# Second attention's follow-up jobs at other steps of its loop, and the mixture layers' normalised rows kept as fp16 halves that DMA transposes for routing and experts

## The chip, the cores and the metric

The kernel runs on one core of one Trainium2 chip. The metric is the device time of one execution in microseconds; lower is better. Three runs of the kernel before gave 951.81, 952.78 and 956.13 us, so its time is 952.78 us.

## The reference

Two layers, each of them a gated cross attention and a gated mixture of experts, on 2048 tokens (8 x 256) of width 256 with a context of 512 rows:

```
x = x + tanh(g_xattn[0]) * attention0(layernorm(x), ctx)     # linear attention with a sigmoid gate
x = x + tanh(g_ffn[0])   * mixture0(layernorm(x))            # 8 experts, best 2, plus a shared expert
x = x + tanh(g_xattn[1]) * attention1(layernorm(x), ctx)     # softmax, 16 heads of 16, q, k, v and weights rounded to 8 bits
x = x + tanh(g_ffn[1])   * mixture1(layernorm(x))            # 16 experts, best 4, plus a shared expert

mixture(x):
    probs = softmax(x @ router.T);  w = top_k(probs), zero elsewhere (layer 0: divided by their sum)
    routed = sum_e w[:, e] * ((silu(x @ gate_e) * (x @ up_e)) @ down_e)            # inner width 176
    shared = sigmoid(x @ s) * ((silu(x @ sgate) * (x @ sup)) @ sdown)              # inner width 704
    return routed + shared
```

## The kernel before, in words

Every engine has its own program, and they meet through semaphores. `at_least(eng, sem, base, n)` (L197) makes an engine wait until a counter has come to base + n; `both` (L284) makes a pair of such counters, one for each mixture layer. Products are exact to nearly fp32: each operand is kept as two fp16 halves, high and low (low = value - high), and `mm3` (L265) adds three fp16 products for each of the two 128-wide parts of the model width.

The stages come one after the other: weights and context, first attention, then for layer 0 routing (L371 to L457), mixture (`ffn_pe`, `ffn_act`, `ffn_dve`, `ffn_pool`, L669 to L1060), then the second attention (`attn1_pe`, `attn1_act`, `attn1_dve`, `attn1_sp`, `attn1_pool`), then routing and mixture of layer 1, then the output.

**Routing.** The 16 tiles of 128 tokens go in 8 pairs. ACT normalises the even tile of a pair (L424), DVE the odd one (L443), into `xnf` as fp32. PE transposes the pair (L380, four fp32 transposes), ACT copies the high half to fp16 (L428), DVE subtracts for the low half (L451), both into `xnT` with the model width on the partitions; PE makes the router's logits from it (L388), DVE scales them (L455). `xnT` is also the shared expert's operand (L778). SP stores the fp32 rows to a table in DRAM (`token_table`, `table_dma`, L632), with the routing weights beside them. From the logits DVE and PE make lists of slots (`route_part_dve`, L603; it begins with MAX8, L465), which run beside the first five steps of the shared expert. `rows_dve` (L564) waits for the stores of rows, since it reuses `xnf`.

**Expert loop.** Slots come in groups of two tiles of 128, each tile of one expert; 20 groups in layer 0, 40 in layer 1 (`NG`). POOL gathers the rows of a group from the table by index (L673), into a ring of `XR` = 4 groups, and a gather waits for the product of the group that held its place (L671). PE transposes the rows (L815, four fp32 transposes), ACT copies the high half (L894), DVE subtracts (L1002); PE does gate and up (L836, twelve products of 352 columns); ACT applies silu (L903); DVE multiplies (L1018); PE transposes the result (L844), ACT and DVE halve it (L907, L1024), PE does down (L852, ten products of 256 columns), DVE copies it out (L1031), SP stores it to the slot table (L658). PE's program handles in step s: the rows' transposes of group s+1, gate and up of s, the result's transposes of s-1, down of s-2. Bank 6 takes the result's transposes, bank 7 the down product. In layer 0 POOL also splits weights of layer 1 into halves between gathers (`split_part`, L1546), and SP loads them (`load_item`, L1539).

**SP's program** is a list in a fixed order (L1594 to L1657): loads, the zeroing of layer 1's slot table in 16 parts (L652), four weight loads (L1644), `table_dma(sp, 0)`, four more loads, `rows_dma(sp, 0)`, loads, the attention's DMA transposes (L1588), `table_dma(sp, 1)`, a wait for the zeroing, `rows_dma(sp, 1)`, the output.

**Second attention.** 128 steps, one for each pair of heads of each tile. In step s PE makes the logits of step s+2 (L1344) into a ring of 5 banks and the weighted sums of step s-4 (L1356); DVE finds the largest logit of each row (L1450); ACT takes exponentials (L1417), and SP transposes them by DMA (L1588). Other work hangs on certain steps, written out by hand as numbers (L1321, `chain_start` L1323, `query_step`, `output_step`): for every two tiles the queries of a later pair (POOL's rows, PE's transposes, ACT's high and DVE's low half, PE's product, DVE's largest value, scale and fractions, POOL's rounding and cutting, PE's transposes back, ACT's copies) and the output of an earlier one (PE's transposes L1365, ACT's high half L1423, DVE's low half L1465, PE's projection, DVE's update of x L1471, and statistics). An engine that comes to such a job before its operand is there waits, with all that is behind it.

## Time and profile before

| what | value |
|---|---|
| median of 3 runs | 952.78 us |
| the profiled execution: its time | 959.28 us |
| its span, first to last instruction | 957.5 us |
| granted TensorE clock, mean | 0.843 of full |
| instructions | 18420 |

Instants in the rows below count from the start of the span. The profiled execution took somewhat longer than the median; sums are made against it and then moved to the median. PE is TensorE's matmul side, PEld its weight loads, DVE VectorE, ACT ScalarE, POOL GpSimd, SP SyncE; SPq and POOLq are their DMA-issuing instructions. A granted clock of 1.00 is 2.4 GHz, 0.50 is 1.2 GHz.

### The profile page before, as it was taken

What the parts mean: (1) busy time and instruction counts of PE and PEld (TensorE: products, weight loads), DVE (VectorE), ACT (ScalarE), POOL (GpSimd) and SP (SyncE); (2) the same over time, 40 slices, a digit from 0 to 9 for tenths busy, and PEclk for the clock granted to TensorE, in tenths of its full rate; (3) what the DMA queues carried; (4) which work ended last, traced back from release to release, by engine and by line L of the source; (5) the groups of instructions that cost most, each with busy time, mean ns of one, the idle gap of its engine ahead of it and who ended that gap; (6) DMA issues with size and microseconds to landing.
All of it is one profiled execution on the core that took longest, in us unless ns stands there. A gap on an engine that the chain in (4) does not pass through costs nothing.

```text
span 957.5 us, 18420 instructions
## 1 busy us (share of the span) xinstructions
PE 746.1 (78%) x5700; PEld 496.1 (52%) x5701; DVE 686.8 (72%) x1825; ACT 443.4 (46%) x1037; POOL 505.3 (53%) x607
## 2 busy tenths in 40 slices
PE   3469749678988797677777777659879999977994
PEld 1258635456664454344444444335657777754563
DVE  4868947756775777988887888738857777734467
ACT  3355335123332233888887878725123444422331
POOL 6284974566636557553554347010054545478883
PEclk9679876789999899697767676657979999978998
DMA  8034444624542213898889988821034444446444
GB/s 287 1 92 157 157 157 147 187 80 142 164 127 89 66 34 81 146 191 160 151 163 168 182 159 162 148 75 40 0 93 137 136 136 140 142 123 143 79 79 141
DMA packets 205754, 121.17 MB, mean 127 GB/s; under 512 B 146476, under 2 KB 197808, under 8 KB 205680
## 3 DMA queue, kind: packets, MB, share of 16 engines
q1 hardware_dynamic: 192816, 91.10, 39.2%
q0 software_dynamic: 12864, 29.14, 12.5%
q8 instruction: 38, 0.62, 0.3%
q14 instruction: 36, 0.29, 0.1%
HBM read 64.16 MB, written 32.98 MB: 101 GB/s over the span
## 4 chain that ended last, share of the span: by engine, by line
PE 35%; DVE 11%; ACT 7%; issue 6%; DVEq 4%; DMA 3%; another core or an unknown queue 2%; POOL 1%; POOLq 0%; ACTq 0%
PE PS L269 18%; PE PS L852 4%; DVE sb_wk L1450 4%; PE PS L791 3%; ACT sb_xnf L1417 3%; DMA sb_xnf<-sb_xnf 3%; PE PS L1344 2%; ACT sb_wkh L1417 2%; PE PS L815 2%; PE PS L844 2%; PE PS L407 1%; DVEq L250 1%; DVE sb_x_sb L942 1%; DVE sb_x_sb L948 1%
## 5 line engine op out<-in xcount | busy, mean ns | idle before, releaser
L673 POOL DMA_INDIRECT sb_xnf<-token_table,sb_ids x120 | 115.8, 965 | 148.7 <-DVE sb_wk L1018 62.8
L1450 DVE TENSOR_SCALAR_CACHE_REDUCE sb_wk<-PS 128x512 f16<-128x512 f32 x256 | 161.9, 684 | 3.8 <-PE PS L1344 3.8
L269 PE MATMUL PS<-sb_xnT,sb_sgu 128*128 128x512 f16 x528 | 129.5, 398 | 1.1 <-DVE sb_lg L455 0.6
L269 PE MATMUL PS<-sb_region,sb_wkh 128*128 x720 | 122.6, 321 | 4.8 <-issue 3.1
L1417 ACT ACTIVATE sb_xnf<-PS,sb_slotv 128x512 int16<-128x512 f32 x128 | 86.8, 689 | 25.5 <-DVE sb_wk L1450 21.4
L875 ACT ACTIVATE sb_wk<-PS 128x512 f32<-128x512 f32 (+1 forms) x48 | 28.6, 596 | 144.6 <-PE PS L269 123.7
L269 PEld LDWEIGHTS PS<-sb_region,sb_wkh 128*128 128x128 f16 x720 | 69.7, 100 | 47.0 <-issue 13.9
L1417 ACT ACTIVATE sb_wkh<-PS,sb_slotv 128x512 int16<-128x512 f32 x128 | 86.6, 690 | 12.4 <-DVE sb_wk L1450 9.6
L852 PE MATMUL PS<-sb_region,sb_wkh 128*128 x600 | 78.3, 277 | 8.9 <-DVE sb_wa L1031 7.3
L269 PEld LDWEIGHTS PS<-sb_xnT,sb_sgu 128*128 128x128 f16 x528 | 53.0, 102 | 60.7 <-issue 10.9
L791 PE MATMUL PS<-sb_sdn,sb_wkh 128*128 128x256 f16 x544 | 70.8, 282 | 17.4 <-DVE sb_wkh L989 15.2
L1018 DVE SCALAR_TENSOR_TENSOR sb_wk<-PS,sb_sm,sb_wk 128x176 f32<-128x176 f32 x120 | 42.6, 396 | 54.2 <-ACT sb_wk L903 41.2
L1344 PE MATMUL PS<-sb_wa,sb_xnf 128*128 128x512 f16 x88 | 43.0, 489 | 44.6 <-ACT sb_wkh L1417 22.2
L894 ACT ACTIVATE sb_wkh<-PS 128x512 f16<-128x512 f32 x60 | 35.8, 596 | 85.4 <-PE PS L815 48.3
L791 PEld LDWEIGHTS PS<-sb_sdn,sb_wkh 128*128 128x128 f16 x544 | 54.2, 101 | 37.5 <-DVE sb_wkh L989 20.1
L903 ACT ACTIVATE sb_wk<-PS 128x352 f32<-128x352 f32 x60 | 27.8, 463 | 95.8 <-PE PS L269 74.1
L981 DVE SCALAR_TENSOR_TENSOR sb_wk<-PS,sb_wk 128x512 f32<-128x512 f32 (+1 forms) x48 | 33.2, 691 | 53.9 <-ACT sb_wk L875 44.0
L852 PEld LDWEIGHTS PS<-sb_region,sb_wkh 128*128 128x128 f16 x600 | 56.7, 99 | 21.9 <-issue 12.6
L1561 POOL TENSOR_TENSOR sb_region<-sb_stg,sb_region 128x704 f16<-128x704 f32 (+1 forms) x32 | 42.9, 1340 | 19.9 <-issue 17.1
L1002 DVE TENSOR_TENSOR sb_wkh<-PS,sb_wkh 128x512 f16<-128x512 f32 x60 | 41.1, 685 | 17.1 <-ACT sb_wkh L894 13.6
L1739 POOL TENSOR_SCALAR sb_xnT<-sb_xnT 128x256 f32<-128x256 f32 x16 | 7.3, 456 | 85.0 <-DVE sb_xnT L1288 85.0
L815 PE MATMUL PS<-sb_idf,sb_xnf 128*128 128x128 f32 x240 | 38.9, 287 | 16.7 <-DMA sb_xnf<-token_table,sb_ids 16.7
(296 smaller groups left out, 1717.3 us busy)
## 6 DMA issues: line engine op xcount, KB each, us to landing
slot_table<-sb_wa SPq DMA_DIRECT2D x60, 256.0 KB
slot_table<-token_table SPq DMA_DIRECT2D x16, 640.0 KB
sb_stg<-gu SPq DMA_DIRECT2D x24, 352.0 KB
sb_stg<-dn SPq DMA_DIRECT2D x24, 256.0 KB
token_table<-sb_xnf SPq DMA_DIRECT2D x16, 256.0 KB, 4.7
sb_stg<-sgu SPq DMA_DIRECT2D x8, 352.0 KB
sb_x_sb<-x SPq DMA_DIRECT2D x1, 2048.0 KB, 12.3
out<-sb_x_sb SPq DMA_DIRECT2D x16, 128.0 KB
```

What stands on the lines that cost most here:

```text
L269: last = nc.tensor.matmul(out_, lhs(i, c), rhs(j, c), start=(c == 0 and n == 0 and not begun), stop=(c == C - 1 and n == 2 and not more))
L673: nc.gpsimd.indirect_dma_start(xg[l][:, 2 * (g % XR) + n, :], None, xw[l][:, :], bass.IndirectOffsetOnAxis(ap=ids[:, 2 * g + n:2 * g + n + ...
L791: last = nc.tensor.matmul(PS[:, first + i // 2, i % 2 * D:(i % 2 + 1) * D], wkh[:, HR * h + v, i * P:(i + 1) * P], sdn[:, j, k, :], start= ...
L815: last = nc.tensor.transpose(PS[:, 4 + s % 2, (2 * n + c) * P:(2 * n + c + 1) * P], xg[l][:, 2 * (s % XR) + n, c * P:(c + 1) * P], idf[:, :])
L852: last = nc.tensor.matmul(PS[:, 7, n * D:(n + 1) * D], wkh[0:r, 4 + 2 * u + i, (2 * c + n) * P:(2 * c + n + 1) * P], DN[l][0:r, bass.ds(e[ ...
L894: nc.scalar.activation(wkh[:, 2 * (s % 2), :], PS[:, 4 + s % 2, :], ACT.Copy).then_inc(e_xh[l].sem, 1)
L1002: nc.vector.tensor_tensor(wkh[:, 2 * (s % 2) + 1, :], PS[:, 4 + s % 2, :], wkh[:, 2 * (s % 2), :], ALU.subtract).then_inc(e_xl[l].sem, 1)
L1018: last = nc.vector.scalar_tensor_tensor(wk1[:, 2 + u, n * EI:(n + 1) * EI], PS[:, 2 * u + n, EI:EG], wv[u][:, n:n + 1], wk1[:, u, n * EI:( ...
L1344: nc.tensor.matmul(PS[:, (2 * s + h) % LB, :], q_iT[t % 3][:, pair, :], keys, start=True, stop=True).then_inc(h_qk, 1)
L1417: nc.scalar.activation(h_count[s % 4][:, h * CTX:(h + 1) * CTX], PS[:, (2 * s + h) % LB, :], ACT.Exp, scale=-1.0, bias=h_nb[u][:, h:h + 1] ...
L1450: nc.vector.tensor_scalar(h_any[(2 * s + h) % 6], PS[:, (2 * s + h) % LB, :], LEVELS, None, ALU.add, ALU.min, accum_out=h_nb[s % 3][:, h:h ...
L1561: nc.gpsimd.tensor_tensor(lo, w, hi, ALU.subtract).then_inc(stg_split[n % 4], 1)
```

## The change

**Rows as halves.** In routing, both engines normalise into `wk1` (ring of four pairs); ACT copies the high half and DVE subtracts the low half as rows, side by side in `xnf` as fp16 (`x_rows`, the same bytes as one fp32 row). SP transposes each pair by one DMA transpose, 128 x 1024 fp16, into `xnT` (seen as `x_cols`), and only after all eight come the stores of rows. PE's logits wait for the transposes; four banks take them, and DVE scales them four pairs later. PE's transposes go.

```diff
+            for j in range(NT // 2):
+                at_least(pe, x_turned[j % 4][l], 0, 16 * (j // 4 + 1))
+                at_least(pe, r_lgc[l], 0, j - 3)
+                for i in range(2):
+                    t = 2 * j + i
+                    last = mm3(PS[:, j % 4, i * n:(i + 1) * n], lambda h, c: x_cols[:, t, h, c, :],
+                               lambda h, c: rw[l][:, h, c, :])
+                last.then_inc(r_lg[l].sem, 1)
...
         def table_dma(sp, l):
             for j in range(NT // 2):
-                at_least(sp, r_xn[l], 0, j + 1)
-                at_least(sp, r_xd[l], 0, j + 1)
+                at_least(sp, r_xh[l], 0, j + 1)
+                at_least(sp, r_xl[l], 0, j + 1)
+                at_least(sp, x_turned[j % 4][l], 0, 16 * (j // 4))
+                sp.dma_start_transpose(x_turns[:, 2 * j:2 * j + 2].rearrange("p t g n -> p (t g) n"),
+                                       x_rows[:, 2 * j:2 * j + 2].rearrange("p t h n -> p (t h n)")).then_inc(x_turned[j % 4][l].sem, 16)
+            for j in range(NT // 2):
                 sp.dma_start(token_rows(xw[l], 2 * j, 2, slice(0, D)), xnf[:, 2 * j:2 * j + 2, :]).then_inc(stored[l].sem, 16)
```

**Expert loop.** The gathered rows are halves already. SP transposes them by DMA, two of 128 x 512 fp16 for each group, into a ring of four (`xT`), four groups ahead of the store of the group's result. PE's four transposes of the rows, ACT's copy and DVE's subtraction go. The result's transposes take two banks in turn (5 and 4), the down product two (6 and 7), and PE's waits on them are one group later. The wait for the zeroing moves behind the first four of layer 1's transposes.

```diff
         def rows_dma(sp, l):
+            def turn(g):
+                at_least(sp, e_ld[l][g % XR], 0, 32 * (g // XR + 1))
+                at_least(sp, e_gu[l], 0, g + 1 - XR)
+                if g == 0:
+                    at_least(sp, s_d[l], 0, HALF)
+                for n in range(2):
+                    sp.dma_start_transpose(xT[g % XR][:, 2 * C * n:2 * C * (n + 1), :],
+                                           xg[l][:, 2 * (g % XR) + n, 0:D].bitcast(F16)).then_inc(e_xT[l][g % XR].sem, 16)
+            for g in range(XR):
+                turn(g)
+            if l == 1:
+                sp.wait_ge(table_zeroed, 16 * ZERO_PARTS)
             for g in range(NG[l]):
+                if g + XR < NG[l]:
+                    turn(g + XR)
                 at_least(sp, e_y[l], 0, g + 1)
                 sp.dma_start(ys[l][2 * g * P:(2 * g + 2) * P, :].rearrange("(n p) d -> p n d", p=P),
                              yb[g % 2].rearrange("p (n d) -> p n d", n=2)).then_inc(e_st[l][g % 2].sem, 16)
...
             def group(base, s):
                 u = s % 2
-                if inside(base, s, 0, NG[l] - 1):
-                    transposes(base, s + 1)
                 if inside(base, s, 0, NG[l]):
                     e = experts(base, s)
-                    at_least(pe, e_xl[l], base, s + 1)
+                    at_least(pe, e_xT[l][s % XR], base * 8, 32 * (s // XR + 1))
...
-                at_least(pe, e_hl[l], base, s - 1)
+                at_least(pe, e_hl[l], base, s - 2)
...
                 if inside(base, s, 2, NG[l] + 2):
                     e = experts(base, s - 2)
-                    at_least(pe, e_y[l], base, s - 2)
+                    at_least(pe, e_hl[l], base, s - 1)
+                    at_least(pe, e_y[l], base, s - 3)
```

**Second attention.** Only the steps at which jobs are issued, and places in `xnT` so that jobs that now overlap have their own.

```diff
-        ROWS, TO_PE, HIGH_Q, LOW_Q, PRODUCTS, LARGEST, SCALES, FRACTIONS, PARTS, BACK, COPIES = 0, 1, 2, 3, 4, 7, 8, 10, 10, 12, 13
+        ROWS, TO_PE, HIGH_Q, LOW_Q, PRODUCTS, LARGEST, SCALES, FRACTIONS, PARTS, BACK, COPIES = 0, 1, 1, 4, 3, 7, 8, 10, 10, 10, 11
...
-            return max((GSTEPS - 1) * (G - 1), GSTEPS * (G - 1) - 4)
+            return max((GSTEPS - 2) * (G - 1), GSTEPS * (G - 1) - 4)
```

Of the output's jobs PE's transposes and ACT's high half go from step 6 to 5, DVE's low half from 7 to 8, PE's projection from 8 and 9 to 7 and 8, DVE's update from 10 to 11, its statistics from 11 and 12 to 12 and 15.

## Rows read from the trace of the kernel before

**Rows 1.** The page: busy time, share of the span and instructions of each engine.

```profile
PE 746.1 (78%) x5700; PEld 496.1 (52%) x5701; DVE 686.8 (72%) x1825; ACT 443.4 (46%) x1037; POOL 505.3 (53%) x607
```

**Rows 2.** Stages: start:end, us, busy of PE, PEld, DVE, ACT, POOL, PEclk, DMA share, GB/s.

```profile
195.00:292.00 97.00, 85.66 (x614) 61.61 (x615) 62.16 (x161) 33.04 (x81) 55.17 (x56) 0.96 0.44 131
373.00:634.00 261.00, 186.14 (x1675) 105.29 (x1673) 213.08 (x648) 201.38 (x543) 116.39 (x178) 0.73 0.85 155
637.00:653.00 16.00, 12.03 (x130) 9.44 (x131) 9.88 (x35) 9.96 (x17) 0.79 (x1) 0.50 0.38 133
...
695.00:845.00 150.00, 142.34 (x1078) 109.45 (x1079) 110.67 (x291) 59.99 (x144) 74.89 (x81) 0.97 0.44 131
845.00:882.00 37.00, 24.41 (x135) 14.84 (x133) 13.32 (x31) 6.26 (x16) 29.68 (x29) 0.77 0.56 130
```

**Rows 3.** Line 1031, DVE's copy of a group's result: layer 0, then layer 1 to 845.

```profile
L1031 DVE COPY sb_wa<-PS x20: 690/692/693, 211.0 to 288.9; 128x512 f32<-128x512 f32 x20
...
L1031 DVE COPY sb_wa<-PS x33: 690/692/692, 717.4 to 843.5; 128x512 f32<-128x512 f32 x33
```

**Rows 4.** The chain of waits in layer 1's expert loop: start, us, what.

```profile
839.90 1.34 PE PS L269 x9
...
841.68 1.10 PE PS L852 x10
842.77 0.44 PE PS L815 x4
```

**Rows 5.** Waits: us in all, times, longest; 205 to 285 (two rows), 705 to 845.

```profile
POOL sb_region L1561 <- issue: 15.1, 6, 3.5
...
POOL sb_xnf L673 <- DVE sb_wk L1018: 1.1, 2, 0.9
...
POOL sb_xnf L673 <- DVE sb_wk L1018: 61.7, 35, 2.8
```

**Rows 6.** Timeline around layer 0's routing: start, us, engine, line.

```profile
154.56 0.17 DVE L455 TENSOR_SCALAR sb_lg<-PS 128x18 f32<-128x18 f32 x1 [0.49 <-PE PS L269]
...
158.37 5.31 SPq L1541 DMA_DIRECT2D sb_stg<-gu  x1
...
165.82 2.26 SPq L637 DMA_DIRECT2D token_table<-sb_xnf  x3
...
169.98 0.78 POOL L1556 TENSOR_SCALAR sb_region<-sb_stg 128x704 f16<-128x704 f32 x1 [13.20 <-DMA sb_stg<-gu]
...
179.51 1.15 DVE L572 TENSOR_TENSOR sb_wa<-sb_region,sb_slotc 128x640 f16<-128x640 f16 x1 [2.34 <-DMA token_table<-sb_xnf]
```

**Rows 7.** DMA, 600 to 622: queue, packets, MB, share; issues to landing; one issue.

```profile
q1 hardware_dynamic: 12764, 3.17, 83.7%
...
sb_xnf<-sb_xnf SPq DMA_TRANSPOSE x7, 3.3
...
606.88 1.23 SPq L1588 DMA_TRANSPOSE sb_xnf<-sb_xnf  x1
```

**Rows 8.** Timeline of layer 1's routing: the first pair, the last logits.

```profile
640.00 0.60 ACT L428 ACTIVATE sb_xnT<-PS 128x512 f16<-128x512 f32 x1 [0.73 <-PE PS L380]
...
640.63 0.69 DVE L451 TENSOR_TENSOR sb_xnT<-PS,sb_xnT 128x512 f16<-128x512 f32 x1 [1.92 <-ACT sb_xnT L428]
...
651.96 0.19 DVE L455 TENSOR_SCALAR sb_lg<-PS 128x34 f32<-128x34 f32 x1 [0.49 <-PE PS L269]
```

**Rows 9.** DMA queues in layer 1's expert loop, 700 to 840: packets, MB, share.

```profile
q0 software_dynamic: 3489, 10.11, 26.9%
q1 hardware_dynamic: 8704, 8.39, 17.4%
```

**Rows 10.** Second attention: DVE's waits, 400 to 620; line 1450, all of it.

```profile
DVE sb_x_sb L1471 <- PE PS L275: 15.4, 7, 3.0
...
DVE sb_xnT L1465 <- ACT sb_xnT L1423: 6.1, 6, 2.5
...
L1450 DVE TENSOR_SCALAR_CACHE_REDUCE sb_wk<-PS x256: 627/685/693, 375.2 to 620.4; 128x512 f16<-128x512 f32 x128
```

More of the change, by code:

```diff
@@ L289, in gated_flamingo @@
         r_xn = both("r_xn", NT // 2)
-        r_xT = both("r_xT", NT // 2)
+        x_turned = [both(f"x_turned{u}", 32) for u in range(4)]
         r_xh = both("r_xh", NT // 2)
@@ L333, in gated_flamingo @@
         e_ld = list(zip(*(both(f"e_ld{u}", 32 * len(range(u, NG[0], XR))) for u in range(XR))))
+        e_xT = list(zip(*(both(f"e_xT{u}", 32 * len(range(u, NG[0], XR))) for u in range(XR))))
         e_st = list(zip(*(both(f"e_st{u}", 16 * len(range(u, NG[0], 2))) for u in range(2))))
@@ L351, in gated_flamingo @@
         yr = [xnf_flat[:, r * 2 * D:(r + 1) * 2 * D].rearrange("p (k d) -> p k d", d=D) for r in range(CR)]
-        y_sum = [w[:, n * D:(n + 1) * D] for w, tiles in ((stg_flat, 8), (wqp32, 4), (xnf_flat[:, 12 * D:16 * D], 4))
+        y_sum = [w[:, n * D:(n + 1) * D] for w, tiles in ((stg_flat, 8), (wqp32, 4), (wkv32, 4))
                  for n in range(tiles)]
@@ L364, in token_rows @@
             return ap[r:r + n * P, cols].rearrange("(n p) d -> p n d", p=P)
+        LOGITS_LATE = 4
         CHOICES = 1
@@ L809, in ffn_pe @@
             at_least(pe, r_ids[l], 0, 1)
-            def transposes(base, s):
-                at_least(pe, e_ld[l][s % XR], base * 8, 32 * (s // XR + 1))
-                for n in range(2):
-                    for c in range(C):
-                        last = nc.tensor.transpose(PS[:, 4 + s % 2, (2 * n + c) * P:(2 * n + c + 1) * P],
-                                                   xg[l][:, 2 * (s % XR) + n, c * P:(c + 1) * P], idf[:, :])
-                last.then_inc(e_xT[l].sem, 1)
             def experts(base, s):
@@ L843, in group @@
                         for c in range(C):
-                            last = nc.tensor.transpose(PS[:, 6, (2 * c + n) * P:(2 * c + n + 1) * P],
+                            last = nc.tensor.transpose(PS[:, 5 - u, (2 * c + n) * P:(2 * c + n + 1) * P],
                                                        wk1[:, 3 - u, n * EI + c * P:n * EI + (c + 1) * P], idf[:, :])
@@ L856, in group @@
                     last.then_inc(e_d[l].sem, 1)
-            transposes(0, 0)
             steps(pe, NG[l] + 2, XR, XR, 3, group)
@@ L890, in ffn_act @@
                     nc.scalar.activation(numbers[l], bc(io[:, 0:P], NT), ACT.Copy).then_inc(r_numbers[l].sem, 1)
-            def high_x(base, s):
-                at_least(act, e_xT[l], base, s + 1)
-                nc.scalar.activation(wkh[:, 2 * (s % 2), :], PS[:, 4 + s % 2, :], ACT.Copy).then_inc(e_xh[l].sem, 1)
             def group(base, s):
                 u = s % 2
-                if inside(base, s, 0, NG[l] - 1):
-                    high_x(base, s + 1)
                 if inside(base, s, 0, NG[l]):
@@ L1013, in group @@
                 if inside(base, s, 0, NG[l] - 1):
-                    low_x(base, s + 1)
+                    weights(base, s + 1)
                 if inside(base, s, 0, NG[l]):
@@ L1093, in gated_flamingo @@
         q_iT = [w.bitcast(F16).rearrange("p (g n) -> p g n", n=P) for w in
-                (*(xnf[:, 12 + 2 * u:14 + 2 * u, :].rearrange("p t d -> p (t d)") for u in range(2)), xn32[:, 10 * D:12 * D])]
+                (*(xnf[:, 12 + 2 * u:14 + 2 * u, :].rearrange("p t d -> p (t d)") for u in range(2)), xn32[:, 14 * D:16 * D])]
         h_h = [wkh[:, 2 * u:2 * u + 2].rearrange("p a b -> p (a b)") for u in range(4)] + \
```

109 lines of the change are left out of this document (47 added, 62 removed).

## The prediction

> **What bounds the kernel now.** I read the busy totals first: no engine is busy all the time, PE the longest [rows 1]. The table of stages then shows why: in the first mixture layer's expert loop (195 to 292 us) and the second's (695 to 845) PE is nearly always busy, at a granted clock of 0.96 and 0.97 of full speed; in the second attention (373 to 634) DVE, ACT and the DMA engines are each between 0.77 and 0.85 busy, and none is full; and where layer 1's tokens are normalised (637 to 653; layer 0's stage is alike) PE runs at clock 0.50, and only 16 us are at stake [rows 2]. The stages follow each other, so what one loses moves the end by as much.
>
> Third, for each loop, who waits. In layer 1 a group takes (843.5 - 717.4)/32 = 3.94 us [rows 3], and PE's links in the chain follow each other without a gap, 0.149 us for a gate/up product, 0.110 for one of the down projection, 0.44 for four fp32 transposes [rows 4]. Twelve, ten and twice four of them are 3.77 us of 3.94: PE is the bound. POOL has slack there: it waits 61.7 us for DVE. In layer 0 a group takes 77.9/19 = 4.10 us by the same rows of the copy, and POOL waits for DVE for 1.1 us only, but 15.1 us ahead of its own third part of a weight split [rows 5]: there POOL, which gathers rows and splits weights in turn, sets the pace, and PE waits for gathers.
>
> **Part 1, routing in layer 0: slower.** This is the largest term. Today the logits need PE transposes, ACT and DVE, and the last is scaled at 154.56 us. The row stores of SP are behind in time: SP is held by the zeroing of the slot table and then by four weight loads until 165.82, when the first store of rows goes out; that it went out so late cost nothing until 179.51, where DVE waited 2.34 us for the stores [rows 6]. The change puts eight DMA transposes in the place of these stores, at the same point of SP's program, and now the logits need them. They can't be issued before 165.82. The queue is backed up too: the load issued at 158.37 landed at 169.98 [rows 6], and three more loads stand behind it, so I let the first transpose run at about 170. One of 128 x 1024 fp16 took 0.837 x 22 us / (3.17 MB / 0.25 MB) = 1.45 us of all 16 DMA engines in the attention, 3.3 us from issue to landing, with 1.23 us on SP's queue [rows 7]. Eight are 11.6 us, so the last is done at about 182, lands by 183, and with PE's last logits and DVE's scale the routing ends near 184: 29.4 us later than 154.56. The 2.34 us wait for the stores goes, since they have some 20 us of route to land in. Net **+26.5**. Bounds: without backlog 1.5 us of SP per transpose gives 165.8 + 8 x 1.23 + 3.3 = 179 (+22); if the loads ahead hold the queue until 173, +31.
>
> **Part 2, routing in layer 1: a little slower.** Here SP is free. ACT and DVE keep their work per pair of tiles (a copy of 0.60 us, a subtraction of 0.69 and a normalising each [rows 8], with SBUF for PSUM as the source); PE loses four transposes, the queue gains 1.45 us per pair. Without PE's step the first low half is ready somewhat ahead of today's 640.63 + 0.69 [rows 8], and its transpose runs from about 640.8; 8 x 1.45 = 11.6 gives 652.4, some 2 us to land and 0.7 for logits and scale: 655 against 651.96 today [rows 8]: **+3**. Bounds 0 (ACT and DVE pace it and the tail is short) and +6. The later row stores are hidden: 30 us of routing follow.
>
> **Part 3, fill of the two expert loops: +2.** A gather lands, then two transposes of half size take 1.45 us of DMA and about 3.3 to land [rows 7], in place of PE's 0.44, ACT's 0.60 and DVE's 0.69 us and the hand-overs between them [rows 4, 8]. One microsecond each; bounds 0 and +4 together.
>
> **Part 4, expert loop of layer 1: faster.** PE loses the four transposes of the rows, 0.44 us per group: 3.94 to 3.50 us. ACT loses a copy of 0.60, DVE a subtraction of 0.69: neither was the bound. The doubled banks for the second transposes and the down product take away waits that hardly show. What takes PE's place is DMA: the queues carried (0.269 + 0.174) x 140 us over 35.5 groups = 1.75 us per group [rows 9]; with 1.45 of transposes it is 3.20 us, 91% of 3.50. The attention held 0.85 over 261 us [rows 2] and never had to be full. The ring of four stands it: from DVE's product of a group to the products four groups on there are two gathers (about 4.5 us), two transposes (3.3 to 4.7), then 1.8, 0.6 and 0.8 for PE, ACT and DVE, 11 to 13 us, or 2.8 to 3.2 per group. On SP's queue a group's two transposes (about 0.65 us each) stand ahead of the store of four groups before, whose data is later than the gather; that costs nothing. I take 3.58 us: 0.36 x 33 groups = **-12**. Bounds -15 (PE alone) and +3 (DMA at 0.85 share sustained: 3.20/0.85 = 3.76, and the end of the loop worse). The 37 us after 845, where DVE, ACT and PE stand still at clock 0.77 [rows 2], I leave alone: no wait there is for what changes.
>
> **Part 5, expert loop of layer 0: +2.** POOL paces it, and POOL's work is the same; PE's 0.44 us there only ends a wait sooner. DMA goes from 0.44 [rows 2] to about 0.44 + 1.45/4.1 = 0.8, and POOL's drains, which stood 15.1 us in six splits, get longer if gathers land later. Bounds -4 (the last groups at PE's pace) and +8.
>
> **Part 6, the attention: faster.** Queue order only. DVE waited for PE at the update 15.4 us in 7 turns, for ACT at the low half 6.1 us in 6 [rows 10]; the change lets PE project a step earlier and DVE take the low half one and the update one step later (and the query chain's low half too). Both waits should go: for 8 turns some 24 us of DVE time. What is late next: DVE's own work. From 375.2 to 620.4 us are 128 steps of 1.92 [rows 10]; DVE is busy 0.82 of the stage and ACT 0.77, DMA 0.85 [rows 2]. Should DMA go no higher than 0.92, then 8% of 245 us, 19 us, is all there is. The new order has PE take the query transposes two steps sooner after POOL has cut them, and PE wait for DVE's low half at a step that DVE reaches later than before; some of the gain goes there. I take **-10**, with bounds -19 and 0.
>
> **The sum.** 26.5 + 3 + 2 - 12 + 2 - 10 = +11.5 us. The profiled execution took 959.28 us around its span of 957.5, so it would be 971 in it; the median of the runs is 952.78, so I predict **964 us**. About 0.5% (4.8 us) is what a measurement of this kernel can tell from no change.
>
> **A rule against a row.** A transpose of 256 KB took 1.45 us of the DMA engines, a store of the same bytes 0.174 x 140 / (8.39 / 0.25) = 0.73 [rows 7, 9]. The Trainium skill (Advanced Engine Details and Errata, X-Bar Transpose) says that transpose DMAs are as fast as regular ones. The row speaks against it.
>
> **Rivals.**
> *The order on SP does not bind layer 0* (the other side). If transposes reached the queue as the halves come, at 141 us and on, routing would cost +3 as in layer 1: 11.5 - 23.5 = -12, 941 us. It decides from a first issue before about 154, where part 1 falls to +15. Against it: SP is busy with zeroing and loads that nothing in the change moves [rows 6]. Chance 0.07.
> *All gains arrive.* PE-bound layer 1 (-15), attention to the DMA's limit (-19), layer 0's end -2: 26.5 + 3 + 2 - 15 - 2 - 19 = -4.5, 948 us (just inside no change). For it: PE's links without gaps [rows 4] and waits that all sit at the moved steps [rows 10]. Chance 0.15.
> *DMA saturates.* Gathers, stores and transposes share 16 engines: layer 1's loop +3, layer 0's +8, attention -5: 26.5 + 3 + 4 + 3 + 8 - 5 = +39.5, 992 us; halfway 978. For it: 91% wanted. Chance 0.14.
> *Transposes at the rate of a store*, 0.73 us: part 1 less 8 x 0.72 = 5.8, part 2 at 0, layer 1 at -15, layer 0 at 0: 20.7 + 0 + 2 - 15 + 0 - 10 = -2.3, 950 us. Against it stands the 1.45 [rows 7]. Chance 0.03. It is what the rule above would give.
> My forecast has 0.61, and its own range is 953 to 974.
>
> **How the numbers follow.** Range 945 to 980: it takes in the forecast, the second and fourth rivals nearly whole and half of the third. Slower by over 0.5% (above 957.5): 0.57 of the forecast and the third rival, 0.71. Within 0.5%: most of the second rival, the fourth, 0.04 of the forecast, 0.18. Faster: the first and a part of the second, 0.11.
>
> **What would show it.** Layer 0: SP issues the first transpose near 166 us, and the first MAX8 of routing comes near 184, not 154.8; if it comes before 160, part 1 is wrong and with it the sign. Layer 1: the normalising and the logits take some 3 us longer than today. Layer 1's groups at 3.5 to 3.65 us, DMA share near 0.9, clock still near 1; if PE waits for DMA there and groups take 3.9 or more, DMA has saturated. Layer 0's groups at 4.1 or more. Attention: no wait at DVE's update, 1.80 to 1.87 us per step; if PE waits for POOL's or DVE's query steps instead, the stall has moved.

## The result and the profile after

The changed kernel takes 1009.92 us (median of four runs, 1004.68 to 1010.55) against 952.29 us for the kernel before (951.72 to 956.13). By the means of the runs it takes 1.058 times as long, interval 1.054 to 1.063; all ratios below are of means too, each against runs of the kernel before on the same chip. The direction was as predicted. The size was not: +57.6 us for a forecast of +11.5, beyond the range's upper end of 980. Two profiles below, g2's and f1's, are of slow executions (1018.94 and 1020.70 us, where the fastest of each took 1003.56 and 1003.02); behind the last gather of rows, outside the stages that are compared, they take 14 and 12 us more than the changed kernel's.

First the page's busy totals and then the table of stages of the changed kernel, in the columns of [rows 2]: both expert loops, the attention, layer 1's normalising, and layer 1's expert loop where it is steady.

```profile
PE 703.5 (70%) x5396; PEld 456.3 (45%) x5397; DVE 647.8 (64%) x1765; ACT 408.1 (40%) x977; POOL 505.0 (50%) x607
...
213.00:322.00 109.00, 79.09 (x546) 54.02 (x545) 54.30 (x147) 21.69 (x61) 57.64 (x59) 0.94 0.69 166
402.00:683.00 281.00, 189.86 (x1666) 109.37 (x1666) 213.93 (x650) 202.83 (x544) 117.44 (x177) 0.71 0.78 144
683.00:700.00 17.00, 3.90 (x96) 3.19 (x96) 8.85 (x24) 9.39 (x17) 0.00 (x0) 0.50 0.82 151
770.00:895.00 125.00, 104.33 (x759) 72.34 (x760) 70.96 (x205) 30.22 (x87) 54.90 (x59) 1.00 0.77 189
```

The change took off what it meant to: 43 us of PE, 39 of DVE, 35 of ACT [rows 1]. But PE, which was busy for 95% of layer 1's loop [rows 2], is now busy for 104.33 of 125 us, 83%. The work left, and holes came. The attention, 261 us before, is 281 us with the same work on DVE and ACT and a DMA share that fell from 0.85 to 0.78.

The copies of the expert groups' results (line 1031 before, 1029 now) and the attention's maxima (line 1450 before, 1448 now) give the time of each stage, as [rows 3] and [rows 10] did:

```profile
L1029 DVE COPY sb_wa<-PS x20: 691/692/693, 232.1 to 317.3; 128x512 f32<-128x512 f32 x20
...
L1029 DVE COPY sb_wa<-PS x30: 691/692/693, 769.7 to 894.3; 128x512 f32<-128x512 f32 x30
...
L1448 DVE TENSOR_SCALAR_CACHE_REDUCE sb_wk<-PS x256: 627/686/693, 402.1 to 665.0; 128x512 f16<-128x512 f32 x128
```

A group of layer 0 takes 85.2/19 = 4.48 us (4.10 before), one of layer 1 124.6/29 = 4.30 (3.94), an attention step 262.9/128 = 2.05 (1.92). The ledger, in us, each stage by its first or last instruction in the two traces:

| stage | before | after | difference | predicted |
|---|---|---|---|---|
| layer 0: first MAX8 of the routing | 154.8 | 184.3 | +29.5 | +29.4 |
| its routing, MAX8 to first gather | 37.2 | 28.7 | -8.5 | -2.3 |
| layer 0's experts and the rest to the attention | 183.2 | 189.1 | +5.9 | +2, +1 of the fills |
| attention, first to last maxima | 245.2 | 262.9 | +17.7 | -10 |
| its end and layer 1's routing to its last MAX8 | 33.0 | 36.4 | +3.4 | +3 |
| last MAX8 to layer 1's last gather of rows | 190.6 | 201.5 | +10.9 | -12, +1 |
| last gather to the end of the span | 113.5 | 105.9 | -7.6 | 0 |

The sum is 51.3 us of span. The last line is put down to the one execution of the kernel before that was profiled: 959.28 us against a median of 952.78, with a stall in its tail (last section). Without it the ledger gives 58.9, near the 57.6 of the medians. The line before it is touched by the same: the profiles with that stall also have the shorter groups in layer 1, so that like with like, as shown below, the loop lost some 5 to 7 us and not all of 10.9.

### The profile page after: what moved, and what is told of

It is laid out like the page before. It is cut to its first block, busy times and chain, and to the rows that moved or that the text cites. A ratio compares the mean times of both kernels' runs of the same rounds, so it can differ in the third digit from the quotient of the medians.

```text
span 1008.8 us, 17861 instructions
## 1 busy us (share of the span) xinstructions
PE 703.5 (70%) x5396; PEld 456.3 (45%) x5397; DVE 647.8 (64%) x1765; ACT 408.1 (40%) x977; POOL 505.0 (50%) x607
## 4 chain that ended last, share of the span: by engine, by line
issue 25%; POOL 22%; PE 19%; POOLq 8%; DMA 7%; SPq 7%; DVE 6%; ACT 2%; DVEq 2%; ACTq 0%
PE PS L269 11%; PE PS L861 4%; POOL sb_region L731 3%; SPq L656 3%; POOL sb_region L1559 2%; POOL sb_xnf L691 2%; DMA sb_xnf<-token_table,sb_ids 2%; POOLq L1558 2%; DMA sb_xnT<-sb_xnf 2%; POOL sb_stg L731 2%; POOLq L1662 2%; DMA sb_wkh<-sb_xnf 2%; SPq L666 2%; PE PS L852 1%; POOL sb_stg L1556 1%
## 5 line engine op out<-in xcount | busy, mean ns | idle before, releaser
L1448 DVE TENSOR_SCALAR_CACHE_REDUCE sb_wk<-PS 128x512 f16<-128x512 f32 x256 | 164.5, 685 | 48.0 <-PE PS L1342 41.1
L269 PE MATMUL PS<-sb_xnT,sb_sgu 128*128 128x512 f16 x528 | 126.1, 391 | 1.1 <-DVE sb_lg L455 0.6
L1016 DVE SCALAR_TENSOR_TENSOR sb_wk<-PS,sb_sm,sb_wk 128x176 f32<-128x176 f32 x120 | 42.6, 396 | 109.5 <-ACT sb_wk L905 109.5
L269 PE MATMUL PS<-sb_region,sb_wkh 128*128 x360 | 62.7, 328 | 43.7 <-DMA sb_wkh<-sb_xnf 32.0
L809 PE MATMUL PS<-sb_sdn,sb_wkh 128*128 128x256 f16 x544 | 68.3, 276 | 14.7 <-DVE sb_wkh L989 12.8
L861 PE MATMUL PS<-sb_region,sb_wkh 128*128 x600 | 76.5, 273 | 2.8 <-DVE sb_wkh L1024 1.7
L269 PE MATMUL PS<-sb_region,sb_xnf 128*128 x360 | 60.4, 319 | 21.4 <-issue 10.8
L269 PEld LDWEIGHTS PS<-sb_region,sb_wkh 128*128 128x128 f16 x360 | 35.0, 101 | 69.0 <-issue 51.1
L861 PEld LDWEIGHTS PS<-sb_region,sb_wkh 128*128 128x128 f16 x600 | 53.9, 97 | 17.2 <-issue 7.2
L269 PEld LDWEIGHTS PS<-sb_region,sb_xnf 128*128 128x128 f16 x360 | 34.0, 99 | 44.8 <-issue 29.1
L269 PE MATMUL PS<-sb_rw,sb_xnT 128*128 128x9 f16 (+1 forms) x192 | 7.7, 173 | 65.1 <-DMA sb_xnT<-sb_xnf 65.1
```

The lines of the kernel that those rows point to most:

```text
L269: last = nc.tensor.matmul(out_, lhs(i, c), rhs(j, c), start=(c == 0 and n == 0 and not begun), stop=(c == C - 1 and n == 2 and not more))
L809: last = nc.tensor.matmul(PS[:, first + i // 2, i % 2 * D:(i % 2 + 1) * D], wkh[:, HR * h + v, i * P:(i + 1) * P], sdn[:, j, k, :], start= ...
L861: last = nc.tensor.matmul(PS[:, 6 + u, n * D:(n + 1) * D], wkh[0:r, 4 + 2 * u + i, (2 * c + n) * P:(2 * c + n + 1) * P], DN[l][0:r, bass.d ...
L1016: last = nc.vector.scalar_tensor_tensor(wk1[:, 2 + u, n * EI:(n + 1) * EI], PS[:, 2 * u + n, EI:EG], wv[u][:, n:n + 1], wk1[:, u, n * EI:( ...
L1448: nc.vector.tensor_scalar(h_any[(2 * s + h) % 6], PS[:, (2 * s + h) % LB, :], LEVELS, None, ALU.add, ALU.min, accum_out=h_nb[s % 3][:, h:h ...
```

## Layer 0's routing, and the experiment on SP's order

SP's own timeline of the changed kernel (start, us, engine queue, line, destination<-source): zeroing of the slot table, four weight loads, the eight transposes, then the row stores.

```profile
140.91 18.14 SPq L656 DMA_DIRECT2D slot_table<-token_table  x4
159.09 7.35 SPq L1539 DMA_DIRECT2D sb_stg<-gu  x4
166.54 15.06 SPq L638 DMA_TRANSPOSE sb_xnT<-sb_xnf  x8
181.65 6.08 SPq L641 DMA_DIRECT2D token_table<-sb_xnf  x8
```

The first transpose goes out at 166.54 (166 predicted, [rows 6] had 165.82), the eight take 15.06 us of the queue, and the first MAX8 comes at 184.3. The backlog that was forecast is there: the first two transposes hold the queue for 3.3 us each, the other six for 1.27. The first lands at 174.4 and the last at 183.5 (183 predicted). The instant was right to 0.1 us, with a little luck: the transposes started later than at 170 and went faster than one in 1.45 us.

**c1_order** calls the transposes right behind the loads of layer 0's experts, and the zeroing behind the whole loop of layer 0:

```
             two_experts(0, s)
-            for n in range(4):
-                zero_slots(sp, 4 * s + n)
+        turn_rows(sp, 0)
         ...
         rows_dma(sp, 0)
+        for n in range(ZERO_PARTS):
+            zero_slots(sp, n)
```

> The changed kernel with layer 0's eight DMA transposes of rows on SP's queue straight after the loads of layer 0's experts, ahead of the four weight loads, and with all sixteen parts of the zeroing after layer 0's expert loop. Theory, SP's order holds the routing: the first transpose is issued near 142 us, the logits end near 158 in place of 184, and the whole is 22 to 29 us shorter than 1009.9, about 984. Rival, the transposes themselves are slow there (DMA busy with loads): the logits end after 170 and less than 15 us come back. If the zeroing costs as much in the stage after the expert loop as it did before, the routing ends near 158 and the whole still gains less than 15.

992.72 us, ratio 1.043 (1.033 to 1.052). The first MAX8 comes at 154.9 (154.8 before), the first gather at 187.4 instead of 213.0: SP's order was the whole of this term. Some of it was lost again: with the zeroing's traffic ahead of the attention's loads, DVE waited once for 10.5 us at the attention's start, and the stage took 270.6 us.

## The attention: five experiments

The part's two gains were to come from waits of DVE at the update and the low half [rows 10]. Both are gone from the table of waits. These are the waits of the changed kernel from 425 to 660 us (who waits, for what; us in all, times, longest):

```profile
DVE sb_wk L1448 <- PE PS L1342: 39.0, 31, 2.8
...
PE PS L1251 <- POOL sb_xnT L1751: 17.4, 7, 3.2
```

Line 1251 is PE's transposes of the query parts back (step BACK), line 1751 is POOL's cut of the query into integers. PE reaches the transposes at step 10 before POOL has cut, stands there for 2.5 us on the mean, seven times, and behind it in PE's order stand the products that DVE's maxima need. DVE's wait moved from the update to the maxima and grew.

**a1_all_steps_old** puts back all steps of queries and outputs and the chain's start; **a2_query_old** only those of the queries and the chain's start; **a3_back_late** only BACK, COPIES and the start; **g2_chain_old** only the start:

```
-ROWS, TO_PE, HIGH_Q, LOW_Q, PRODUCTS, ..., BACK, COPIES = 0, 1, 1, 4, 3, ..., 10, 11
+a1, a2: 0, 1, 2, 3, 4, ..., 12, 13    a3: 0, 1, 1, 4, 3, ..., 12, 13
-            return max((GSTEPS - 2) * (G - 1), GSTEPS * (G - 1) - 4)
+            return max((GSTEPS - 1) * (G - 1), GSTEPS * (G - 1) - 4)     (all four)
-output_step(s, 5), 7 + j, 5, 8, 11, 12 + 3 * j
+output_step(s, 6), 8 + j, 6, 7, 10, 11 + j     (a1 only)
```

> The changed kernel with every job of the second attention back at its step of before (only the places in memory stay new). Theory, the steps are to blame: the attention, from DVE's first to last search for the largest logit, took 245.2 us before and 262.9 after; here it is 244 to 248 again and the whole about 18 us shorter than the changed kernel's 1009.9, some 992. Rival, the rest of the change (places, DMA, clock) slowed it: it stays at 258 or more and the whole near 1010.

> Only the query chain's steps (from ROWS to COPIES, and the start of the chain) back; the output's jobs stay at their new steps. Theory, PE now comes to the query transposes before POOL has cut the queries, and that is the whole loss, while the output's new steps do what was forecast: the attention takes 228 to 238 us, less than the 245.2 of before, and the whole is 980 to 986. Rival, the projection two steps after the transposes makes PE wait for DVE's low half: the attention stays above 250.

> Query transposes and copies back at steps 12 and 13 and the chain's start at 15 per group as before; the query's high half (1), low half (4) and product (3) and all output jobs stay new. If the early transposes back are the loss: the attention is as in the run with the whole query chain old, within 3 us. If PE's wait for the query's low half at step 3 costs too: it is slower than that run by the difference, 5 us or more.

> The changed kernel with the chain's start of before ((GSTEPS - 1) * (G - 1)) and all else as changed, BACK and COPIES at 10 and 11. If the early transposes back, which come before POOL has cut the query, are the loss: attention 262 as after, ratio 1.055 to 1.06. If it is the denser chain: attention 245 as with both taken back, ratio 1.04. (The other half, the new start with BACK at 12, can't be had: groups then overtake one another's buffers.)

| kernel | attention, us | ratio to before |
|---|---|---|
| the changed kernel | 262.9 | 1.058 (1.054 to 1.063) |
| g2: chain's start old | 259.8 | 1.051 (1.042 to 1.059) |
| a3: and BACK, COPIES at 12, 13 | 245.1 | 1.039 (1.033 to 1.045) |
| a2: and high half, low half and product old | 237.5 | 1.029 (1.024 to 1.035) |
| a1: and outputs old | 242.5 | 1.038 (1.028 to 1.049) |

Read as differences of the stage: the earlier BACK and COPIES cost 14.7 us, the denser chain 3.1, the low half behind the product (with the earlier high half, which a2 moves too) 7.6, and the output steps gain 5.0. Each stage is of one profile, a1 to a3 on one chip and g2 on another, so the 3.1 and the split that g2 makes are the least sure. The row of g2 that decides is the same wait, still there with the old start of the chain:

```profile
PE PS L1251 <- POOL sb_xnT L1751: 15.6, 9, 3.2
```

In a3 it is gone. The other half alone, the new start with BACK at 12, has no run: the query groups would then need one another's buffers in a circle.

**a4_before_outputs_2** is the kernel before with the six output steps of the change and nothing else.

> The kernel before with the new steps of the output's jobs in the second attention and nothing else of the change. The run with all steps old took 242.5 us for the attention, the one with these steps 237.5: so 5 us less than before, ratio 0.995 (0.990 to 0.999). If the gain belongs to the new places in memory or to the change in the mixture, the ratio is 1.00.

943.77 us against 951.95, ratio 0.990 (0.986 to 0.994): it beats both kernels, the kernel before by 1%. Its maxima run from 375.0 to 613.4, 238.4 us instead of 245.2, and the two waits of [rows 10] fell from 15.4 us in 7 turns and 6.1 in 6 to one each from 400 to 640 us:

```profile
DVE sb_x_sb L1471 <- PE PS L275: 3.3, 1, 3.3
...
DVE sb_xnT L1465 <- ACT sb_xnT L1423: 1.8, 1, 1.8
```

## The expert loops: ten experiments

The chain in layer 1's loop of the changed kernel (start, us, what). Line 269 is gate and up, 852 the hidden transposes, 861 down:

```profile
823.50 0.44 PE PS L852 x4
823.94 1.18 PE PS L861 x10
825.12 0.66 issue
825.77 1.96 PE PS L269 x12
```

PE's blocks are 1.96, 0.44 and 1.10 to 1.18 us, and a hole of about 0.6 us stands ahead of gate and up, where before the four transposes stood and the chain had no gap. Two theories. A: the operand is late (gather, SP's queue, landing). B: the hole is TensorE's reading of the two expert numbers into registers (line 832 now, 822 before), which stands right ahead of gate and up and was covered by the transposes.

The read of this group is in the trace, on the side of the weight loads (min, median, max ns, first and last start):

```profile
L832 PEldq TENSOR_LOAD <-sb_texp x1: 761/761/761, 824.9 to 824.9; - x1
```

It runs from 824.9 to 825.6, and gate and up start at 825.77. That is B. There are two such reads a group; over 28 groups in the steady part they took, in the kernel before, in the changed kernel, and in two of the kernels below, b1 and b2:

```profile
L822 PEldq TENSOR_LOAD <-sb_texp x56: 535/547/840, 726.7 to 834.7; - x56
...
L832 PEldq TENSOR_LOAD <-sb_texp x56: 538/782/1032, 775.7 to 893.6; - x56
...
L830 PEldq TENSOR_LOAD <-sb_texp x56: 535/546/906, 765.6 to 874.7; - x56
...
L839 PEldq TENSOR_LOAD <-sb_texp x56: 536/667/994, 774.7 to 888.2; - x56
```

Times per group below are 28 intervals of the copies in the steady part (4.27 us for the changed kernel). One code's loop is not always as long: that of the kernel before took 3.94 us in its profile and 4.10 in a4's, that of the changed kernel 4.27, 4.21 to 4.24 in a1 to a3, and 4.13 in g2. The short ones, 3.94 and 4.13, are from profiles with the stall of the last section. So like with like the loop lost 0.11 to 0.19 us a group (4.21 to 4.27 against 4.10, 4.13 against 3.94), and not the 0.36 between the two profiles above. Where possible, kernels are compared within one chip.

**b1_no_turns_2** leaves out the transposing DMAs after the first four groups (all later groups take the rows of the first four again), **b5_one_turn_2** one of each group's two, **b2_aside_2** sends layer 1's to a place that nobody reads, from a source that is long ready:

```
             for g in range(NG[l]):
-                if g + XR < NG[l]:
-                    turn(g + XR)
```

> The changed kernel with DMA transposes of rows for the first four groups of each mixture layer only; the products of all later groups read these four again, so the routed part of the output is made from the wrong rows. Everything else, the gathers too, stays. Theory A, the operand comes late (SP issues two transposes of 1.26 us and a store per group in a fixed order, and DMA has to land them): without them PE never waits at gate and up, and layer 1's groups fall from 4.15 us (steady part) to 3.5 to 3.6. Theory B, PE's own program is the limit: it loads the experts' numbers into registers ahead of gate and up, which the four transposes of before covered, and the 0.6 us hole ahead of gate and up stays: 4.0 us or more. In layer 0 by theory A 4.48 falls to the 4.1 of before or below.

> As the changed kernel, but in layer 1 the DMA transposes of groups 4 to 39 read constant weights and write to unused memory, at the same instants and of the same size, and PE reads the first four groups' operands again (so layer 1's routed part is made from wrong rows). Same DMA and SP work as the changed kernel, no dependence of PE on it. If it is PE's dependence on late transposes: 3.5 to 3.7 us per group. If it is the DMA load (gathers and stores slowed by the transposes): 4.1 us as in the changed kernel.

> The changed kernel with one DMA transpose per group in place of two: the second tile's product reads the first tile's rows, so the routed part is made from wrong rows for every second tile. SP is busy 1.26 + 0.36 us per group instead of 2.9, DMA 0.73 us less. If the time from a store to the landing of the transposes behind it sets the pace: each group loses a third of 1.26 us or more, 3.7 us or less per group in layer 1. If PE's register loads do it: 4.0 or more.

On one chip: 3.95 us without transposes (ratio 1.040, 1.036 to 1.044), 4.09 with one (1.049, 1.046 to 1.053), 4.11 with both aside (one run, 1006.2 us), and 4.10 for a4, whose loop is that of before. Neither theory stands alone. Most of the hole is there with no transposing DMA at all (B): against a4, b1 is rid of PE's transposes, 0.44 us a group, and gains 0.14. The hole grows with the transposes' traffic though nothing waits for it: 0.16 us. The rows of the reads show how: their mean is 0.61 us in b1 and 0.70 in b2, two a group, which is the 0.16. In layer 0, b1 took 3.92 us a group for 4.48.

**e1_loads_before_turns** reads both pairs of numbers between gate/up and the hidden transposes, **e2_loads_after_turns** between these and down, **e3_loads_no_turns** is e1 without transposing DMAs:

```
         def group(base, s):
+            e = experts(base, s - 2) ...
+            e_next = experts(base, s + 1) ...
             (hidden transposes of s - 1; e2: the two reads stand here)
             (down of s - 2, with e)
+            gate_up(base, s + 1, e_next)
```

> The changed kernel with TensorE's two loads of expert numbers moved: both pairs (down's of the group two back, gate and up's of the next group) are read between a group's gate and up products and its hidden transposes, so that neither stands between down's ten products and the next gate and up. State of the theories: layer 1's groups took 3.945 us before (717.4 to 839.7, 31 intervals), 4.297 after (769.7 to 894.3, 29), 3.943 without the operand transposes (764.7 to 883.0, 30), 4.107 with one a group or with both aside; PE's work is 1.96 + 0.44 + 1.10 = 3.50, and without any transposing DMA a hole of 0.45 still stands ahead of gate and up. Theory B (the hole is the loads' register time, covered before by four transposes, and longer the busier the DMA is): the hole goes, groups 3.55 to 3.7, span shorter by 40 x 0.5 + 20 x 0.4 = 28 us, ratio 0.972 of after, near 1.029 of before. Theory A (the hole is the operand that comes late through gather, SP's turn and landing): groups stay at 4.2 to 4.3, ratio 1.058 of before.

> As the run before, but both pairs of numbers are read after the hidden transposes, right ahead of down. If a load needs only cover by whatever TensorE has queued, this place is as good: 3.55 to 3.7 a group. If what covers it must be long (two microseconds of gate and up rather than 0.44 of transposes), a hole of 0.2 to 0.5 opens ahead of down and groups take 3.8 to 4.1. Theory A: 4.2 to 4.3.

> The first of these two with the transposing DMAs after the first four groups left out, so that the routed part is worked out from wrong rows. It bounds what the loop can reach with the loads covered: theory B 3.50 to 3.6 a group in layer 1 and the same in layer 0 where TensorE's clock is full; the difference to the run with the transposing DMAs is what their queue, landing and traffic cost then. If groups stay at 3.94, the hole is neither the operand nor the place of the loads, and both theories fall.

The hole follows the reads. PE's waits from 773 to 887 us, of e1 (line 854 is the hidden transposes) and then of e2 (862 is down); nothing is left at gate and up:

```profile
PE PS L854 <- issue: 13.1, 26, 1.3
...
PE PS L854 <- DVE sb_wk L1020: 1.4, 1, 1.4
```

```profile
PE PS L862 <- issue: 16.5, 22, 1.6
...
PE PS L862 <- DVE sb_wkh L1028: 7.1, 4, 1.9
```

4.07 us a group in e1, 4.46 in e2, 3.91 in e3; ratios 1.054 (1.050 to 1.059), 1.064 (1.059 to 1.068) and 1.032 (1.027 to 1.036). So it is the reads, but neither place hid them: my 3.55 to 3.7 was wrong. Twelve products of 0.15 us ahead of them did not cover them.

**f1_no_loads** has constant expert numbers (every group uses the last two experts) and no reads; **f2_before_no_loads** is that on the kernel before; **f3_loads_by_four** reads the twelve numbers of a turn of the loop at once; **f4_neither** is f1 without transposing DMAs after the first four groups:

```
-            return nc.values_load_multi_w_load_instructions(texp[0:1, j], ...)[1]
+            return E[l] - 2, E[l] - 1          (f1, f2, f4)
+            if s % XR == 0:                    (f3)
+                v = read(bass.ds(base * 2 + 2 * (s - 2), 2 * (XR + 2)))
```

> The changed kernel with constant expert numbers in both expert loops (the last two experts for every group, so that the routed part is worked out with wrong experts), hence no loads of numbers into TensorE's registers. If the loads are the hole (0.7 us a group in layer 1): groups of 3.50 to 3.65 there and 3.5 to 3.7 in layer 0 where the clock is full, 25 to 40 us off the span, ratio 1.02 to 1.03 of before. If the hole is the operand's way (gather, SP's turn, landing) after all, groups stay above 4.0.

> The kernel before with the same constant numbers. If its four operand transposes covered the loads, little is won: groups of 3.945 become 3.88 to 3.94 (its work is 1.96 + 0.44 + 1.10 + 0.44 = 3.94 with ends that overlap), ratio 0.99 to 1.0. If the loads cost TensorE their time wherever they stand, groups fall by 0.4 or more and the ratio is below 0.98.

> The changed kernel with the numbers of one turn of the loop (four steps, and the two ahead of them for down) read in one load of 12 registers at the turn's first gate and up; three steps in four have no load. If a load's cost is a latency each time: a hole of 1 to 1.5 us in every fourth step, groups of 3.75 to 3.95 on the mean, some 15 to 20 us off the span. If it goes by the number of registers, 12 against 16 a turn: 4.1 to 4.2.

> The changed kernel with constant expert numbers and without the transposing DMAs after the first four groups (routed part worked out from wrong experts and wrong rows). With the loads and the transposes a group of layer 1 took 4.28, without the transposes 3.94, without the loads 4.23. If these two are all that held the loop above TensorE's own 3.50, groups take 3.50 to 3.55, the ratio is 1.00 to 1.02 of before, and TensorE is busy for over 98% of the loop. If a third thing holds it (the chain through ACT and DVE back to TensorE), groups stay above 3.7.

The copies of g2 (the change's own expert loop, same chip), f1, f3 and, on another chip, f4:

```profile
L1029 DVE COPY sb_wa<-PS x29: 691/692/694, 772.6 to 888.2; 128x512 f32<-128x512 f32 x29
```

```profile
L1027 DVE COPY sb_wa<-PS x29: 691/692/694, 786.2 to 892.9; 128x512 f32<-128x512 f32 x29
```

```profile
L1039 DVE COPY sb_wa<-PS x29: 691/692/695, 775.1 to 884.1; 128x512 f32<-128x512 f32 x29
```

```profile
L1025 DVE COPY sb_wa<-PS x29: 691/692/694, 760.1 to 860.0; 128x512 f32<-128x512 f32 x29
```

Over 28 intervals: 4.13 us with reads and transposes, 3.81 without reads, 3.89 with reads by four, 3.57 with neither. The reads are worth about 0.3 us a group and the transposing DMAs another 0.24. f1's figure is the least steady: by which 28 intervals are taken it is 3.78 to 4.01, f3's is 3.80 to 3.91, the other two move by 0.04 at most. So f1 and f3 can't be told apart. f1 also spares TensorE the addresses worked out from the numbers, which f3 keeps, so that f3's 0.24 is the reads alone.

A third limit is left. The chain of f2, the kernel before without reads, is PE's own work and nothing else (line 842 is the hidden transposes there, 850 down, 815 the rows' transposes):

```profile
807.01 1.79 PE PS L269 x12
808.80 0.44 PE PS L842 x4
809.24 1.10 PE PS L850 x10
810.34 0.44 PE PS L815 x4
```

Without the last line it is 3.33 us, and f4 is 0.24 above that. Between the first of its hidden transposes and of its down products PE takes 0.60 us in f4 and 0.44 in f2: there it waits for ACT and DVE, which halve the result. That f4 comes to the 3.58 that I had forecast for the whole change is chance. In f1 the limit that stood behind the reads comes forward. Its waits at gate and up name the DMA, and its chain runs through SP's queue (lines 666: a half-size transpose, 676: the store of a group):

```profile
829.49 0.36 SPq L676
...
829.95 1.22 SPq L666
831.17 0.04 issue
831.21 1.27 SPq L666
832.48 0.04 issue
832.52 0.58 SPq L676
```

```profile
PE PS L269 <- DMA sb_wkh<-sb_xnf: 8.2, 6, 3.3
...
PE PS L269 <- DMA sb_xnf<-sb_xnf: 3.8, 4, 1.2
```

So theory A is true as well, one step behind B. A group wants 0.4 to 0.6 + 1.22 + 1.27 us of SP's queue, about 3 us.

The control on the kernel before: f2 took 3.76 us a group where [rows 3] had 3.94, ratio 0.990 (0.985 to 0.995), so even there the reads cost, 0.17 us. Against a4's 4.10 it would be 0.33; f2's profile has the stall, as the one of before, so I take the 0.17. The ratios of f1, 1.047 (1.042 to 1.051), f3, 1.052 (1.047 to 1.058), and f4, 1.022 (1.018 to 1.026), fell short of what was expected of them: the last six groups took 33 to 40 us in these profiles for 20 in the changed kernel's (last section), and the attention's and layer 0's losses are all still in. f1's layer 0 even took 4.75 us a group for 4.48.

**Two sums of parts.** **c3_query_old_loads** joins a2, e1 and c1 with the zeroing put right behind layer 0's transposes; **h1_outputs_loads** is a4 with f3's reads by four.

> The change's parts that earn, put together: the output steps new, the query steps and the chain's start as before, layer 0's eight row transposes issued right after the loads of layer 0's experts, the zeroing of the slots behind them and ahead of the weights' items (not in the attention as in the run that moved it there, whose first stretch had a stall of 10.5 us), and the loads of expert numbers early. From after's 1009.9: query steps -29.6 as measured, routing -25.6 at the first gather of layer 0 as measured, and by theory B -28: 927 us, ratio 0.973 (0.96 to 0.99). By theory A: 955, ratio 1.003.

> The kernel before with the output jobs' new steps (alone 0.9898 of before) and with the expert numbers of four steps read in one load. Taking the loads away on the kernel before gave 0.9895 (3.855 a group in layer 1 against 3.945). If the reads by four win half of that and it adds up: ratio 0.985 (0.980 to 0.990). If one load of twelve registers opens a hole as long as those it replaces: 0.990 to 0.993.

c3 took 1035.3 us, ratio 1.087 (1.083 to 1.092), the slowest of all. Its timeline of SP says why:

```profile
156.39 80.07 SPq L658 DMA_DIRECT2D slot_table<-token_table  x16
236.52 7.33 SPq L1545 DMA_DIRECT2D sb_stg<-gu  x4
243.90 6.46 SPq L643 DMA_DIRECT2D token_table<-sb_xnf  x8
```

The sixteen pieces of zeroing, 5 us of queue each, spread between weight loads in the kernel before, now stand together ahead of the row stores that the routing waits for, and TensorE, DVE, ACT and POOL all stand still from 180 to 240 us. The rest went as its parts: attention 234.4 us, 4.07 a group. h1 took 951.21 against 959.82, ratio 0.990 (0.986 to 0.994), no more than a4 alone. Its groups took 3.80 us and its last gather of rows came at 835.4, 6.4 us before a4's, but its tail took 114.0 us for a4's 106.8, with the stall of the last section in it.

## Why the prediction was wrong

**Part 1** (layer 0's routing, +26.5): the mechanism and its instant were right (184, measured 184.3; c1 undoes it). The term was too large by 5.5, since I let only the 2.34 us of one wait go. The route itself became 8.5 us shorter. The wait is gone, and DVE's same 117 instructions take 23.67 us of it for 29.98, where POOL, which splits weights, is busy for 1.09 us instead of 15.26. Of line 572's two, one took 1147 ns before and 479 the other, and 484 and 492 after. That POOL is the cause was not tested.

**Part 2** (+3) and **part 3** (+2): right, +3.4 and within what can't be told from the loops.

**Part 4** (layer 1's experts, -12) failed, and with a wrong sign: +10.9 in the ledger, some 5 to 7 like with like. The step was "twelve, ten and twice four of them are 3.77 us of 3.94: PE is the bound", from which I took the 0.44 of the transposes off. By that sum PE's work without them is 3.33 us. The other 0.17 us was there to be read, was left unexplained, and stayed in the 3.50. It was the part of the register reads that stuck out from under the transposes (f2: 3.76 without reads). With the transposes gone about 0.3 us of them stuck out, and behind them the operand came late: 4.27 us a group where I forecast 3.58. A second step was "about 0.65 us each" on SP's queue for a half-size transpose: it took 1.26, as much as the full size in [rows 7]. A third was to let DMA cost nothing below a share of 0.85 to 0.92: its share was 0.77 in the changed kernel's loop, yet the transposes' traffic cost 0.16 us a group where nobody waited for them (b2), by longer reads.

**Part 5** (+2): 4.10 to 4.48 us a group, +7.3 over 19 groups, by the same things: 3.92 without the transposes. My upper bound of +8 held it.

**Part 6** (attention, -10) failed with a wrong sign, +17.7, and is the largest miss. I costed the outputs' steps and let the queries' go along ("some of the gain goes there"). By themselves the output steps gain 5.0 (a2 against a1) to 6.8 us (a4), with the waits that I named. Three moves of the queries' steps cost 25 us together. The one that matters was in the text, "PE take the query transposes two steps sooner after POOL has cut them", but without asking whether POOL has cut by then, and POOL has not.

The rival "DMA saturates" came nearest in size, 992, but not by its mechanism. The rule of the Trainium skill (Advanced Engine Details and Errata, X-Bar Transpose), that such transposes run as fast as regular DMAs, fails in the loop too. In [rows 9] 17.4% of 140 us are 24.4 us for 32 stores of 256 KB, 0.76 us each (I had divided by 35.5 groups, and got 0.73 by taking 8.39 MB as 33.6 stores). From 770 to 895 us the hardware queue has 50.1% of 16 engines for 29 stores and 58 transposes: (62.6 - 22.0)/29 = 1.4 us for a group's two transposes, which carry 256 KB between them, 1.8 times a store.

```profile
q1 hardware_dynamic: 40545, 15.54, 50.1%
q0 software_dynamic: 2784, 8.08, 26.5%
```

## What to carry to other kernels

Work that is taken off the bounding engine is worth its time only if nothing hid beneath it. Add up the engine's instructions per turn and explain what is left over, register reads and branches above all, for they show as a gap only once their cover is gone; then ask what is second in line, here SP's queue. When a step of a software pipeline is moved earlier, look up the instant at which its producer is done now, for each step by itself, and try the moves one by one: here one of the four paid, three cost. And one profile of each side is not enough for a difference of 0.2 us a turn: the same loop came out at 3.94 and at 4.10.

## What the runs showed of the hardware

**Reading numbers into TensorE's registers.** One read of two numbers takes 0.53 us at least, 0.55 in the median without transposing traffic and 0.78 beside it (rows of the reads above). Two of them a group cost TensorE about 0.3 us beside that traffic (g2 against f1) and 0.38 without it (b1 against f4, two chips). Behind twelve queued products both together still cost 0.26 (e1 against f1, two chips), and behind four transposes 0.64 (e2 against f1, two chips); all three comparisons with f1 carry its unsteadiness. With one read of twelve numbers every four groups the loop is 0.24 us shorter than g2's (f3). The Trainium skill (DMA: Bandwidth & Descriptors, Latency and other measured facts) gives about 600 ns as the floor of a `tensor_load` and says that the compiler unrolls fourfold to amortise it. The traces agree nearly: 0.53 us is below that floor, and reading by four did pay.

**A transposing DMA's issue does not shrink with its size.** 128 x 512 of fp16 held SP's queue as long as 128 x 1024 (min, median, max ns):

```profile
L666 SPq DMA_TRANSPOSE sb_wkh<-sb_xnf x60: 1188/1260/1987, 217.3 to 900.9; - x60
...
L638 SPq DMA_TRANSPOSE sb_xnT<-sb_xnf x16: 1232/1270/3367, 166.5 to 695.1; - x16
```

**A stall at the loop's exit in some executions.** In the profile of before, and in f1 to f4, g2 and h1, the first groups behind layer 1's loop stand: two results come 12.2 and 10.2 us after the one ahead of them in the kernel before, 18.5 and 10.3 in g2. The chain of the kernel before has it as

```profile
849.92 7.23 another core or an unknown queue
...
857.21 5.06 another core or an unknown queue
```

The last six groups take 32 to 43 us with it and 18 to 21 without (after, a4, b1, e1). POOL's gathers of the sums, whose last is issued 99 us after the last gather of rows in both traces, run beside it, so that the end moves by less: from that last gather to the end it is 109.5 to 120.4 us with the stall, 105.9 to 107.1 without. All six profiles from two of the chips have it (f1 to f4, g2, h1), on which the kernel before took 960 us, and none from the other three, where it took 952. What is waited for, and why only some have it, stays open.
